# A wait on VectorE's decay scan ahead of GpSimd's low part of the system, in a gated delta-rule layer

## The reference

```
q, k, v = silu(causal_conv4(x @ Wq)), silu(causal_conv4(x @ Wk)) / sqrt(128), silu(causal_conv4(x @ Wv))
a, b = sigmoid(x @ Wa + ba), sigmoid(x @ Wb + bb)          # one decay and one strength per head and token
for each token:                                            # state S: 128 x 128 per head and sequence
    err = S k - v
    S = a * S - b * err k^T
    o = S q
o = layernorm(o) * ln_w + ln_b;  out = (o * sigmoid(x @ Wg)) @ Wo
```

## Time and profile before

| | before |
|---|---|
| runs | 2385.12, 2385.58, 2389.96 us |
| median | 2385.58 us |
| profiled execution, span from first to last instruction | 2385.5 us |
| PE busy | 2299.3 us (96%) |
| PEld busy (weight loads, beside PE) | 1756.6 us (74%) |
| DVE busy | 2051.2 us (86%) |
| ACT busy | 1989.9 us (83%) |
| POOL busy | 1892.8 us (79%) |
| the chain that ended last | PE 67%, DVE 13%, ACT 7% |

### The profile page before, as it was taken

One profiled execution on the slowest core, in us unless ns is written; L12 is line 12 of the kernel. 1 busy time (PEld: TensorE's weight loads), 2 busy tenths in 40 slices (PEclk: granted clock), 3 DMA queues, 4 the chain that ended last, 5 costly groups with the idle time before them and its releaser, 6 DMA issues.

```text
span 2385.5 us, 65201 instructions
## 1 busy us (share of the span) xinstructions
PE 2299.3 (96%) x25520; PEld 1756.6 (74%) x25520; DVE 2051.2 (86%) x4283; ACT 1989.9 (83%) x3956; POOL 1892.8 (79%) x2063
## 2 busy tenths in 40 slices
PE   5999999999999999999999999999999999999999
PEld 2555777777777777777777777777777777777765
DVE  8789998888888888888999888888888888899654
ACT  3877888888888888888888888888888888889865
POOL 4875788888888888888888888888888888889875
PEclk8999999999999999999999999999999999999999
DMA  5441111111121111111111011101210121111001
GB/s 141 129 144 57 34 33 24 33 33 33 29 63 42 33 30 27 33 33 32 47 50 42 24 33 33 33 24 33 68 38 28 33 53 33 28 33 33 17 28 45
DMA packets 72849, 103.65 MB, mean 43 GB/s; under 512 B 21472, under 2 KB 33760, under 8 KB 72416
## 3 DMA queue, kind: packets, MB, share of 16 engines
q1 hardware_dynamic: 72544, 99.48, 16.0%
HBM read 85.69 MB, written 13.77 MB: 42 GB/s over the span
## 4 chain that ended last, share of the span: by engine, by line
PE 67%; DVE 13%; ACT 7%; issue 2%; POOL 1%; DVEq 0%; ACTq 0%; POOLq 0%
PE bank L3174 21%; DVE a_prod L1614 5%; DVE k_rows L1712 5%; PE bank L3104 4%; PE bank L3145 4%; PE bank L3090 4%; PE bank L3105 4%; PE bank L3244 3%; PE bank L2996 3%; PE bank L3010 3%; PE bank L3008 3%; PE bank L2924 2%; PE bank L2926 2%; PE bank L2925 2%; PE bank L2970 2%
## 5 line engine op out<-in xcount | busy, mean ns | idle before, releaser
L1712 DVE SCALAR_TENSOR_TENSOR k_rows<-bank,k_prm,k_rows 128x509 f32<-128x509 f32 (+2 forms) x1152 | 819.9, 736 | 1.6 <-ACT k_rows L2286 0.2
L3174 PE MATMUL bank<-k_z,k_kqv 128*128 128x512 f16 x2304 | 617.9, 380 | 38.9 <-DVE k_rows L1712 37.8
L2378 ACT ACTIVATE k_wide<-bank 128x512 f16<-128x512 f32 x640 | 378.9, 592 | 64.9 <-PE bank L3010 60.5
L1644 DVE TENSOR_TENSOR k_y<-bank,k_masks 128x256 f16<-128x256 f32 x768 | 305.8, 411 | 97.8 <-PE bank L2996 97.1
L2286 ACT ACTIVATE k_rows<-bank,k_prm 128x512 f32<-128x512 f32 x384 | 300.7, 783 | 69.0 <-PE bank L3174 68.8
L1331 POOL TENSOR_TENSOR k_narrow<-k_narrow,k_rows 128x512 f32<-128x512 f32 x128 | 171.0, 1336 | 157.9 <-ACT k_narrow L2412 157.9
L3174 PEld LDWEIGHTS bank<-k_z,k_kqv 128*128 128x128 f16 x2304 | 178.7, 98 | 147.5 <-DVE k_rows L1712 49.3
L2296 ACT ACTIVATE k_rows<-k_rows 128x512 f32<-128x512 f32 x384 | 220.9, 620 | 68.3 <-DVE k_rows L1712 68.1
L2996 PEld LDWEIGHTS bank<-k_wide 128*128 128x128 f16 x3072 | 180.9, 98 | 100.7 <-ACT k_wide L2361 7.2
L3010 PE MATMUL bank<-k_wide,k_y 128*128 128x64 f16 x3072 | 251.7, 193 | 0.6 <-DVE k_y L1644 0.6
L1232 POOL TENSOR_TENSOR k_wide<-k_solve,k_ident 128x512 f16<-128x512 f32 x128 | 163.2, 1275 | 103.4 <-DVE k_solve L1623 103.0
(11 more groups left out here) (171 smaller groups left out, 6613.3 us busy)
## 6 DMA issues: line engine op xcount, KB each, us to landing
a_decay<-decay_rows SPq DMA_DIRECT2D x128, 258.0 KB, 3.5
k_solve<-cumulative_rows SPq DMA_DIRECT2D x96, 258.0 KB, 3.4
weight_pairs<-k_wide SPq DMA_DIRECT2D x15, 512.0 KB, 2.9
k_kqv<-weight_pairs SPq DMA_DIRECT2D x9, 512.0 KB, 4.9
stream<-in_L_attn_x SPq DMA_DIRECT2D x8, 512.0 KB, 7.6
out<-stream SPq DMA_DIRECT2D x7, 512.0 KB, 2.9
k_rows<-in_L_attn_Wk SPq DMA_DIRECT2D x4, 512.0 KB, 4.8
k_rows<-in_L_attn_Wq SPq DMA_DIRECT2D x4, 512.0 KB, 5.0
```

What stands on the lines that cost most here:

```text
L1644: nc.vector.tensor_tensor(even(y16[:, j], mb), bank[LEV[par]][:, 0:U * C // 2].rearrange("p (u b m) -> p u b m", u=U, m=mb), masks[:, j].r ...
L1712: nc.vector.scalar_tensor_tensor(out=dst[:, d:S], in0=bank[PJ[j % 2]][:, 0:S - d], scalar=prm[:, i, U * (n // B) + j, TAPS - 1 - d:TAPS - ...
L2378: nc.scalar.activation(both, bank[LEV[par]][:, :].rearrange("p (two b m) -> p two b m", two=2, m=mb), ACT.Copy).then_inc(m[f"act_lev{par}" ...
L3174: mm = pe.matmul(bank[PJ[j % 2]][:, :], wt, z16[:, zh, k, cols], start=(x == 0), stop=(x == 5))
```

## The change

`system_low(t)`, outside the edges, waits until `dve_scan` stands at t + 2, that is until the scan of step t+1 has ended. That is the scan that stands in VectorE's stream at the time when GpSimd comes to `system_low(t)`. `scaled_q`, which follows in GpSimd's stream, comes behind it, and so does everything after that. No instruction is added, removed or moved in any stream.

```
--- before.py
+++ after.py
@@ -1251,6 +1251,8 @@
             par = t % 2
             if edge(t):
                 pool.wait_ge(m["pool_am"], t + 1)
+            else:
+                pool.wait_ge(m["dve_scan"], t + 2)
             nc.gpsimd.tensor_tensor(al16[:, par], at[:, :, :], am16[:, par],
                                     ALU.subtract).then_inc(m["pool_al"], 1)
```

## The result

The changed kernel takes 2417.11 us in the median (2416.78 to 2417.4), against 2385.77 for the kernel before on the same chip: a ratio of 1.0128 over all runs (1.0131 between the medians), with a 95% interval of 1.0114 to 1.0142. It is slower by 31 us, inside the range, 5 us above the forecast of 2412. The profiled execution has a span of 2415.1 us, 29.6 more than the profile before.

A forecast was written before the change was run, and what follows sets the result against it. TensorE was taken as at work in nearly all of a 63.75 us round. 28 rounds longer by 0.87 us give 24.4, two odd stretches 2.1: 26.5 on 2385.5 makes 2412.0 us, range 2398 to 2428.

The forecast's parts named there:

- The estimate by that rule alone: Scans in stretches 0 and 3 shorten by 1.06 and 1.0 us over 28 rounds: 58 us returned, 2328.
- The prediction's cap of 45: TensorE's stalls behind `check_solution`, 0.94 us in stretch 0 and 0.67 in stretch 3, allow 1.61 a round, 45 at most.
- The chain: From the scan's start through GpSimd's five instructions to TensorE's `first_inverse`: 7.38 us, 7.34 to 7.46 by the bounds.
- The stretches: Steady loop from one decay scan to the next, 0 to 3 by chunk, four a round; a round grows by 0.87 us.
- The cover of stretch 2: TensorE's 0.26 us stall behind `first_inverse` covers the 0.14 growth there; uncovered, 4 us in all.
- the two odd early stretches: In two early rounds stretch 0 was already short, its scan first; each grows by 1.03 us, 2.1 in all.
- The freed time came through: Rival: TensorE finds the mask ready at `first_inverse`, the round gains 1.61 us, 45 in all, 2340; chance 0.05.
- The scan did not stay long: Rival: something else keeps the scan at 2.2 us, costing 2.9 us a round, 2469; chance 0.03.
- Transfers: `load_cum` is issued 3.68 us behind the scan's start, lands at 6.7 to 7.1, before `scaled_k` at 7.28; costed at nothing.
- the point at which lateness decides: Rival of late cumulative decays: landings from some 5 us hold the next scan; at 6.0, 56 us more, 2468; chance 0.05.
- The base of the sum: The 26.5 us were added to the profiled 2385.5 us, taken as the median of the runs, 2385.58.

The follow-up runs named there:

- the exchange without a wait: The kernel before with the calls `scaled_q` and `system_low` exchanged and no wait on the scan: 2362.09 us, ratio 0.9889.
- the versions with a shorter chain: Only `scaled_q` or only `system_low` behind the wait: 2341.74 us (built on the kernel before) and 2339.86 (built on the changed kernel); latter waiting in stretches 0 and 3 alone, 2339.13.

## Why the prediction was right

**What excludes what.** This is shown. Scans take 1.22 us wherever GpSimd stands still, and the exchange without a wait has both orders of the same pair. The Trainium skill, "SBUF — State Buffer", section "Who interferes with whom", states the exclusive lock between a VectorE instruction with two SBUF inputs and a GpSimd instruction that reads SBUF, given to the first for its whole length; the rows agree (2.22 against 1.22 on the one side, 2.15 against 1.16 on the other). The estimate by that rule alone, 2328, missed by 89 us and in sign, because it has nothing of what stands behind the GpSimd instruction that is held back. Where the chain leaves room, the rule's gain is cut to TensorE's stalls: 47 to 50 us of the 58. The prediction's cap of 45 (1.61 a round) was a little low, because TensorE's stream was not packed behind that stall: `correction` (L3079) starts 1.19 us behind that projection before (1229.76 to 1230.95), where its weight load waits for VectorE, and 1.10 (1207.14 to 1208.24) with the wait behind `system_low`. Those 0.09 us in stretch 0, and as much in stretch 3, are what 1.78 has over 1.61.

**The chain.** This is shown too. 7.38 us were summed, 7.37 and 7.38 measured; the spacings that no row showed back to back came out as 1.14 (1260.06 to 1261.20) and 1.23 (1261.20 to 1262.43), where 1.14 and 1.24 were taken. `system16` to the mask took 1.37 instead of 1.35, so the sum is exact to 0.01 in part because small errors cancel.

**The stretches.** -0.02, +0.85, 0 and +0.04 were forecast, and the round grew from 63.75 to 64.66, 0.91 instead of 0.87. Stretch 1 alone carries 0.86; that it is stretch 1 is shown by the two experiments that leave the wait out of it or keep it only there. The cover of stretch 2 held (15.70), and the two odd early stretches grew by 0.92 and 1.04 us, where 1.03 was taken for each: the one at 399.01 was not quite alike (16.03 us before, with a scan of 1.34).

**The rivals.** The freed time came through in the versions with a shorter chain, where `first_inverse` on TensorE finds its mask in time: the condition that the rival named, met by taking one instruction out. 2340 us was its price, 2339 to 2342 was measured. In the changed kernel it was not met. The scan did not stay long anywhere that the wait reaches.

**Transfers.** This term was mis-sized, and by the prediction's own words a `scaled_k` that waits for its transfer is a sign of being wrong: 29 of them waited. The load was costed at nothing, with landings of 3.0 to 3.4 us, and the point at which lateness decides was put at landings of some 5 us, by way of the next scan. But the change itself brings the two loads closer together, 0.37 us apart instead of 1.04, and the load then takes 3.7 to 3.8 us in the median in stretches 0 and 3, and 5.0 at worst; in that worst case a load of weights follows as well, where the prediction saw nothing else large on the queue. The point is also nearer: 0.69 us of lateness, by way of `query_low` and TensorE's Gram matrix. In the profiled run seven stretches are too long for this reason by 0.16 to 0.73 us, 2.4 in all, each with a `scaled_k` more than 0.69 late. That is most of the 3.1 us that this run's span lost beyond the sum.

**The base of the sum.** The 26.5 us were put on a profiled span of 2385.5 us, as if that were the median run of 2385.58. But in all runs whose span is on record, the time is 1.7 to 1.9 us more than the span (2416.78 and 2415.1 for the profiled run of the changed kernel), so the agreement to 0.1 us was chance: by this, the execution profiled before was some 1.6 us slower than the median one. These 1.7 us and the 3.1 above make nearly all of the 5.1 by which the forecast was low.

## What to carry to other kernels

When two engines exclude each other, a wait can choose which one stands still, but everything behind the waiting instruction stands still with it: follow the waiting engine's queue to the next engine that needs something from it, and compare that with the stall that is to go. Place the wait so that as little as possible lies between it and that hand-over; here one instruction less behind the scan turned a loss of 1.2% into a gain of 2%. And leave the wait out where the two don't meet, if the chain there has no room.

## What the runs showed of the hardware that was not expected

- A lead of 0.03 us decides which of the two runs at its own length: the scan at 1.22 us and GpSimd at 2.15, or GpSimd at 1.16 and the scan at 2.22, in stretches 0 and 3 of the same round. With a lead of 0.51 us and 0.65 of GpSimd's instruction left, the scan took 1.74.
- The same load of 258 KB took, in the median of stretches 0 and 3 of the loop, 3.2 us with another issued 1.04 us behind it, 3.2 with that one 2.4 us ahead, and 3.6 to 3.8 with it 0.37 behind. With the other 0.43 ahead it took 4.0 us in stretch 1 of the kernel before, and 3.2 to 3.3 in the same stretch of the changed kernel and its repeat, with it 2.4 ahead.
- In the worst case shown, 5.0 us, a load of weights followed as third within 1 us; that the third caused it was not tried.
